# A transformer block on one core: powers of two moved to VectorE's PSUM bank, and the order of its start and end rebuilt

## What is computed

```
q, k, v = split(x @ Wqkv.T + bqkv)            # 16 heads of 16
q = elu(q * scale) + 1 ; k = elu(k * scale) + 1
y = q * cumsum(k * v) / max(sum_head(q * cumsum(k)), 1e-3)
x = layernorm(x + y @ Wproj.T + bproj)
h = gelu(bq(x) @ bq(w_fc).T + b_fc)           # 1024 wide
x = layernorm(x + bq(h) @ bq(w_proj).T + b_proj)
bq(v): blocks of 32; s = 2^(floor(log2(max|v|)) - 3); round(v / s) * s
```

## Time and profile before

| | us |
|---|---|
| median of 3 runs (lowest, highest) | 286.66 (284.94, 287.47) |
| the profiled execution, its own time | 287.42 |
| its span | 285.6 |
| VectorE busy | 242.0 (85%) |
| TensorE matmul busy | 245.0 (86%) |
| ScalarE, GpSimd busy | 146.4, 154.8 |
| TensorE's mean granted clock | 0.94 |
| chain that ended last | VectorE 52%, TensorE 24%, GpSimd 8%, DMA 8% |

### The profile page before, as it was taken

One profiled execution on the slowest core, in us unless ns is written; L12 is line 12 of the kernel. 1 busy time (PEld: TensorE's weight loads), 2 busy tenths in 40 slices (PEclk: granted clock), 3 DMA queues, 4 the chain that ended last, 5 costly groups with the idle time before them and its releaser, 6 DMA issues.

```text
span 285.6 us, 3556 instructions
## 1 busy us (share of the span) xinstructions
PE 245.0 (86%) x1156; PEld 143.7 (50%) x1156; DVE 242.0 (85%) x505; ACT 146.4 (51%) x238; POOL 154.8 (54%) x113
## 2 busy tenths in 40 slices
PE   6798897899999999999999999999999989276460
PEld 5544564564565546564656455645664456131230
DVE  1299699599999999999999999999999999848622
ACT  0662317465648564847484747475648554208002
POOL 1055154567628763876377647673676377627501
PEclk9999599999999999999999999999999999759666
DMA  6910020206320662066205720483055302530542
GB/s 165 364 60 3 0 55 21 39 0 147 73 39 0 157 138 40 0 147 147 39 0 117 161 56 1 72 187 73 0 54 134 72 1 40 146 73 0 110 110 73
DMA packets 55793, 22.26 MB, mean 78 GB/s; under 512 B 45280, under 2 KB 55520, under 8 KB 55776
## 3 DMA queue, kind: packets, MB, share of 16 engines
q1 hardware_dynamic: 54144, 21.77, 33.8%
q10 hardware_dynamic: 1632, 0.27, 0.6%
HBM read 7.35 MB, written 4.19 MB: 40 GB/s over the span
## 4 chain that ended last, share of the span: by engine, by line
DVE 52%; PE 24%; POOL 8%; DMA 8%; issue 4%; ACT 2%; SPq 1%; ACTq 0%; POOLq 0%; DVEq 0%
DVE vbank L788 10%; PE abank L1030 9%; DVE vbank L766 6%; PE dbank L1082 6%; DVE hq L703 6%; POOL num L352 4%; DMA h<-in_L_ffn_w_fc_dram 4%; DVE kvsum L744 3%; DMA xqT<-xq 3%; DVE r L760 3%; DVE vbank L778 3%; DVE r L800 3%; POOL rstd L357 2%; PE bbank L1041 2%; DVE y L756 2%
## 5 line engine op out<-in xcount | busy, mean ns | idle before, releaser
L1030 PE MATMUL abank<-xT,WqkvT 128*128 128x512 f32 x176 | 83.5, 610 | 5.7 <-DVE kf L727 4.0
L372 POOL TENSOR_TENSOR h_round<-h,h_inv 128x1024 f16<-128x1024 f32 x32 | 69.1, 2158 | 17.3 <-DVE h_inv L698 15.5
L504 ACT ACTIVATE h<-hbank 128x512 f32<-128x512 f32 x64 | 36.8, 600 | 65.2 <-PE hbank L1073 65.0
L1030 PEld LDWEIGHTS abank<-xT,WqkvT 128*128 128x128 f32 x176 | 31.6, 193 | 37.8 <-issue 23.8
L1082 PE MATMUL dbank<-w_prT,hT 128*128 128x256 bf16 x256 | 38.1, 299 | 7.9 <-DMA hT<-hq 7.8
L348 POOL TENSOR_TENSOR qk<-qf,ksum 128x512 f32<-128x512 f32 x16 | 22.6, 1413 | 31.0 <-DVE ksum L739 18.6
L788 DVE TENSOR_REDUCE vbank<-h 128x32 f32<-128x1024 f32 x32 | 38.9, 1214 | 0.5 <-ACT h L504 0.5
L1073 PE MATMUL hbank<-w_fcT,xqT 128*128 128x512 bf16 x128 | 38.3, 381 | 0.0
L498 ACT ACTIVATE expz<-abank,zbias_neg 128x512 f32<-128x512 f32 x30 | 20.6, 687 | 32.0 <-PE abank L1030 31.6
L357 POOL TENSOR_TENSOR rstd<-vareps,minus_half 128x4 f32<-128x4 f32 x16 | 16.1, 1008 | 36.2 <-DVE vareps L774 36.2
L1082 PEld LDWEIGHTS dbank<-w_prT,hT 128*128 128x128 bf16 x256 | 26.7, 106 | 17.4 <-DMA hT<-hq 9.5
(11 more groups left out here) (91 smaller groups left out, 347.9 us busy)
## 6 DMA issues: line engine op xcount, KB each, us to landing
x_sb<-in_L_attn_x_dram SPq DMA_DIRECT2D x8, 512.0 KB, 4.8
out_dram<-o_sb SPq DMA_DIRECT2D x7, 512.0 KB, 3.2
h<-in_L_ffn_w_fc_dram SPq DMA_DIRECT2D x1, 1024.0 KB, 10.3
h<-in_L_ffn_w_proj_dram SPq DMA_DIRECT2D x1, 1024.0 KB, 11.5
Wqkv_sb<-in_L_attn_Wqkv_dram SPq DMA_DIRECT2D x1, 512.0 KB, 6.6
hT<-hq SPq DMA_TRANSPOSE x32, 3.0
out_dram<-o_sb SPq DMA_DIRECT2D x4, 128.0 KB, 1.7
Wqkv_sb<-in_L_attn_Wqkv_dram SPq DMA_DIRECT2D x1, 256.0 KB, 7.0
```

Of the source, the lines that this page charges most:

```text
L372: nc.gpsimd.tensor_tensor(h_round[:, t % 2].rearrange("p (g j) -> p g j", j=BLOCK_K), h[:, t].rearrange("p (g j) -> p g j", j=BLOCK_K), h_ ...
L504: nc.scalar.activation(h[:, t, half * HALF:(half + 1) * HALF], hbank[half][:, :], ACT.Gelu).then_inc(s_h, 1)
L1030: last = nc.tensor.matmul(ps[:, :], WqkvT[:, k, e * P:(e + 1) * P], xT[:, k], start=(k == 0), stop=(k == CC - 1))
```

## The change

1. *Powers in PSUM.* `powers` gives way to `paired_powers` for x and h (the weights keep the old one): the exponent bits go once to SBUF (`x_exp`, `h_exp`), the inverse is made from them, and a third instruction multiplies them by 65537 into 32-bit words in `vbank`, each word two equal bf16. `times_power` reads these words as pairs of bf16. `quantise_x` and `quantise_h` wait for one more semaphore.
2. *Start.* q's and k's weights are loaded apart, k first; x is transposed first, then k's, q's; ScalarE runs one Exp on four elements before anything else; `split_biases` goes ahead of `w_exponents(0)`; `quantise_w(0)` and others change places; chunk 0's xq is turned by TensorE and copied by ScalarE.
3. *Order in the steady loop.* On VectorE, TensorE, ScalarE, GpSimd and SP's queue, as the diff shows.
4. *Last chunk.* LayerNorm 1, x's quantisation, LayerNorm 2 and the last stores go by halves of two tiles (new helpers `..._half`); xq and hq of chunk 7 are turned by TensorE and copied by ScalarE instead of by DMA; `residual_2(7, 1, 0)` waits for `norm_2(6)` explicitly.

The core of the diff (the written-out steps 5 and 6 follow the loop's pattern and are left out, the `_half` helpers are the old ones on two tiles):

```diff
-        x_pow = sb("x_pow", [P, TILES * XB, 2], BF16)
+        x_exp = sb("x_exp", [P, TILES * XB], BF16)
...
-        h_pow = sb("h_pow", [P, TILES, HB, 2], BF16)
+        h_exp = sb("h_exp", [P, TILES, HB], BF16)
...
+        x_pow, h_pow = vbank[:, 168:168 + TILES * XB], vbank[:, 360:360 + TILES * HB]
...
-            sp.dma_start(Wqkv_sb[:, 0:4], Wqkv_d[:, 0:4]).then_inc(s_wqk, 16)
+            sp.dma_start(Wqkv_sb[:, 2:4], Wqkv_d[:, 2:4]).then_inc(s_wk, 16)
+            sp.dma_start(Wqkv_sb[:, 0:2], Wqkv_d[:, 0:2]).then_inc(s_wq_in, 16)
             sp.dma_start(Wqkv_sb[:, 4:6], Wqkv_d[:, 4:6]).then_inc(s_wv, 16)
...
-            load(3)
             turn_hq(0, 2)
             turn_hq(0, 3)
-            turn_xq(1)
+            load(3)
 
             def step(s):
                 n = s + 1
+                turn_xq(n)
                 turn_hq(n, 0)
-                turn_hq(n, 1)
                 n = s
...
+                turn_hq(n, 1)
                 n = s + 4
                 load(n)
                 n = s + 1
                 turn_hq(n, 2)
...
-            turn_hq(7, 0)
-            turn_hq(7, 1)
-            turn_hq(7, 2)
-            turn_hq(7, 3)
             store(6)
...
                 n = s + 2
                 q_times_ksum(n, n % 2, 0)
                 n = s + 1
...
                 round_h(n, 2)
+                round_h(n, 3)
 
             for s in range(STEPS):
                 step(s)
...
             round_h(6, 2)
-            scale_shift_1(7)
             round_h(6, 3)
-            round_x(7, 1)
+            scale_shift_1_half(7, 0)
+            scale_shift_1_half(7, 1)
+            round_x_half(7, 1, 0)
+            round_x_half(7, 1, 1)
             scale_shift_2(6)
             round_h(7, 0)
             round_h(7, 1)
             round_h(7, 2)
             round_h(7, 3)
-            scale_shift_2(7)
+            scale_shift_2_half(7, 0)
+            scale_shift_2_half(7, 1)
...
+            def load_table():
+                act.wait_ge(s_half, 1)
+                nc.scalar.activation(table[:, :], minus_half[:, :], ACT.Exp).then_inc(s_table, 1)
...
+            def copy_xqT_first(n):
+                act.wait_ge(s_xqT_ps, 1)
+                nc.scalar.copy(xqT[:, :, :, :].rearrange("p t c n -> p (t c n)").bitcast(U32), hbank[0][:, :].bitcast(U32)).then_inc(s_xqT, 16)
+
+            def copy_xqT_half(n, g):
+                act.wait_ge(s_xqT_ps, g + 2)
+                nc.scalar.copy(xqT[:, 2 * g:2 * g + 2].rearrange("p t c n -> p (t c n)").bitcast(U32),
+                               abank[g][:, 0:C].bitcast(U32)).then_inc(s_xqT, 16)
+
+            def copy_hT(n, t):
+                slot = (4 * n + t) % HT
+                act.wait_ge(s_hT_ps, t + 1)
+                wait(act, s_down, 4 * n + t + 1 - HT)
+                nc.scalar.copy(hT[:, slot].rearrange("p c n -> p (c n)").bitcast(U32), abank[t % 2][:, :].bitcast(U32)).then_inc(s_hT[slot], 16)
...
+            load_table()
             copy_xT(0, 0, abank[0])
+            copy_wqkT(0, hbank[0])
+            copy_xT(0, 1, abank[1])
+            copy_wqkT(1, hbank[1])
+            activate(0, 1, 0, abank[0])
             copy_wvT()
-            copy_xT(0, 1, abank[1])
+            activate(0, 0, 0, hbank[0])
             copy_wprojT()
-            activate(0, 1, 0, abank[0])
-            activate(0, 0, 0, hbank[0])
             activate(0, 1, 1, abank[1])
             activate(0, 0, 1, hbank[1])
...
             def step(s):
                 n = s
+                gelu(n, 3, 0)
+                gelu(n, 3, 1)
+                n = s + 2
+                copy_xT(n, 0, abank[0])
+                copy_xT(n, 1, abank[1])
+                activate(n, 1, 0, abank[0])
+                activate(n, 0, 0, abank[1])
+                n = s + 1
+                norm_1(n, n % 2)
+                n = s + 2
+                activate(n, 1, 1, abank[1])
+                activate(n, 0, 1, abank[0])
+                n = s + 1
+                gelu(n, 0, 0)
+                gelu(n, 0, 1)
+                n = s + 2
+                widen_rec(n)
+                n = s + 1
+                gelu(n, 1, 0)
+                gelu(n, 1, 1)
                 gelu(n, 2, 0)
                 gelu(n, 2, 1)
-                gelu(n, 3, 0)
-                gelu(n, 3, 1)
-                n = s + 2
-                activate(n, 1, 0, abank[0])
-                activate(n, 0, 0, abank[1])
-                n = s + 1
-                norm_1(n, n % 2)
-                n = s + 2
-                activate(n, 1, 1, abank[1])
-                activate(n, 0, 1, abank[0])
-                n = s + 1
-                gelu(n, 0, 0)
-                n = s + 3
-                copy_xT(n, 0, abank[0])
-                n = s + 1
-                gelu(n, 0, 1)
-                n = s + 2
-                widen_rec(n)
-                n = s + 1
-                gelu(n, 1, 0)
-                gelu(n, 1, 1)
                 n = s
                 norm_2(n)
-                n = s + 3
-                copy_xT(n, 1, abank[1])
 
...
+            norm_1_half(7, 1, 0)
+            norm_1_half(7, 1, 1)
+            copy_xqT_half(7, 0)
             gelu(7, 0, 0)
             gelu(7, 0, 1)
             gelu(7, 1, 0)
+            copy_xqT_half(7, 1)
             gelu(7, 1, 1)
             gelu(7, 2, 0)
             gelu(7, 2, 1)
-            norm_2(6)
             gelu(7, 3, 0)
             gelu(7, 3, 1)
-            norm_2_last(7)
+            copy_hT(7, 0)
+            norm_2(6)
+            copy_hT(7, 1)
+            copy_hT(7, 2)
+            copy_hT(7, 3)
+            norm_2_half(7, 0)
+            norm_2_half(7, 1)
...
+            def paired_powers(amax, exp, inv, pow2, s_amax, s_exp, s_inv, s_pow, n):
+
+                top = amax.bitcast(U16).rearrange("p (g o) -> p g o", o=2)[:, :, 1]
+                wait(dve, s_amax, n)
+                nc.vector.tensor_scalar(exp.bitcast(U16), top, EXPONENT_BITS, None, ALU.bitwise_and).then_inc(s_exp, 1)
+                wait(dve, s_exp, n)
+                nc.vector.tensor_scalar(inv.bitcast(U16), exp.bitcast(U16), -1.0, float(TO_GRID), ALU.mult, ALU.add).then_inc(s_inv, 1)
+                nc.vector.tensor_scalar(pow2.bitcast(U32), exp.bitcast(U16), float((1 << 16) + 1), None, ALU.mult).then_inc(s_pow, 1)
...
                 nc.vector.tensor_reduce(h_amax[:, t], h[:, t].rearrange("p (g j) -> p g j", j=BLOCK_K), AX_X,
                                         ALU.max, apply_absolute_value=True).then_inc(s_hamax, 1)
-                powers(h_amax[:, t], h_pow[:, t], h_inv[:, t], HB, s_hamax, s_hexp, s_hinv, 4 * S + t + 1)
+                paired_powers(h_amax[:, t], h_exp[:, t], h_inv[:, t], h_pow[:, t * HB:(t + 1) * HB], s_hamax, s_hexp, s_hinv, s_hpow, 4 * S + t + 1)
 
             def quantise_h(S, t):
                 wait(dve, s_hround, 4 * S + t + 1)
-                times_power(hq[:, t], h_round[:, t % 2], h_pow[:, t], HB).then_inc(s_hq, 1)
+                wait(dve, s_hpow, 4 * S + t + 1)
+                times_power(hq[:, t], h_round[:, t % 2], h_pow[:, t * HB:(t + 1) * HB].bitcast(BF16).rearrange("p (g o) -> p g o", o=2), HB).then_inc(s_hq, 1)
...
+            split_biases()
             w_exponents(0)
-            split_biases()
...
 
             def step(s):
+                n = s + 1
+                mean_var_1(n)
                 n = s
-                h_exponents(n, 3)
-                quantise_h(n, 2)
                 residual_2(n, n % 2, 0)
+                quantise_h(n, 3)
                 n = s + 2
                 feature(n, 1, 0, abank[0])
                 sum_k(n, n % 2, 0)
                 feature(n, 0, 0, abank[1])
                 n = s
-                quantise_h(n, 3)
+                residual_2(n, n % 2, 1)
+                n = s + 1
+                x_exponents(n, n % 2)
                 n = s + 2
                 multiply_kv(n, 0, abank[0])
-                n = s + 1
-                x_exponents(n, n % 2)
-                n = s
-                residual_2(n, n % 2, 1)
-                n = s + 2
-                sum_kv(n, n % 2, 0)
-                feature(n, 1, 1, abank[1])
-                n = s + 1
-                quantise_x(n)
                 n = s
                 residual_2(n, n % 2, 2)
                 n = s + 2
+                feature(n, 1, 1, abank[1])
+                n = s + 1
+                quantise_x(n)
+                n = s + 2
+                sum_k(n, n % 2, 1)
+                n = s
+                residual_2(n, n % 2, 3)
+                n = s + 2
                 feature(n, 0, 1, abank[0])
-                sum_k(n, n % 2, 1)
+                sum_kv(n, n % 2, 0)
                 multiply_kv(n, 1, abank[1])
                 n = s
-                residual_2(n, n % 2, 3)
                 mean_var_2(n)
                 n = s + 2
...
             residual_1(7, 1, 0)
-            h_exponents(6, 2)
             quantise_h(6, 1)
+            h_exponents(6, 3)
             residual_1(7, 1, 1)
-            mean_var_1(7)
```

(102 more changed lines are left out.)

312 lines of the change are left out of this document (175 added, 137 removed).

## The result

The change is faster: a median of 272.6 us over four runs (271.57 to 275.36) against 287.07 over four runs of before (284.94 to 288.98), a ratio of 0.951, 95% interval 0.941 to 0.961. In a later series the same kernel gave 272.34 over six runs against 285.61 over ten, 0.953 (0.949 to 0.957). The forecast was 274. Ratios leave out the runs that are more than 1.5% above the fastest of their kernel, which matters in experiment 1 alone. The profiled execution took 271.57 us, the fastest of its four; its span is 269.8: 15.8 us less than the 285.6 of before, where the medians differ by 14.5.

A forecast was written before the change was run, and what follows sets the result against it. VectorE and TensorE were taken to fill the middle steps, with idle time only at both ends. Gains of 6 (start), 0 (middle) and 7 (end) make 13 us off 287.42; with the median 0.76 lower, forecast 274, range 269 to 278.

The forecast's parts named there:

- the second y: Start, projection behind the denominators: done 4.4 us earlier than 35.3 if TensorE's clock falls again, 6.5 if not.
- w_fc's landing and 3.1 us of VectorE work set the start, not PE: Start: k is projected in time, so the first `feature` can start at 15.8, 4.1 us earlier.
- The tight place at the inverse of the next chunk's first tile: Middle step: VectorE's inverse would come while GpSimd still multiplies by kvsum, losing 0.4 us.
- claim (d): Theory stated before the experiments: the middle's 0.25 us loss a step is the third instruction and the blocked inverse.
- The other place, `x_exponents`: Middle step: comes 3.8 us after LayerNorm 1's statistics, now 6.3, leaving a margin of 0.2 us.
- the rival at 292.6 us: Multiply with a PSUM operand falls to one element per cycle, +0.53 us each, 18.6 us in all; chance 0.13.
- GpSimd's 0.38 us: Each of some 27 GpSimd roundings gets 0.38 us shorter with powers in PSUM; priced at nothing in the middle.
- To the end of down(7,0): End, from first product to first down: 5.0 us now, 3.7 to 4.6 new, about 0.8 gained.
- The 1.7 us that the forecast took off for the clock: End: terms summed to 8.7 us gained, taken as 7 because TensorE's clock might be at its lower level.
- The middle gives back: Rival: waits at `x_exponents` and the inverse, or an unoverlapped third instruction, cost 1.1 us a step, 280.6 us; chance 0.17.
- The ends gain little: Rival: lower TensorE clock through both ends, start 4 and end 4 us gained, 278.7 us; chance 0.13.
- It doesn't do what it says: Rival: `h_round` stays at 2.28 us, colliding with the exponents' SBUF instructions, not the multiply; 275.5 us; chance 0.05.

The follow-up runs named there:

- experiment 1: Kernel before with only the bias split moved ahead of `w_exponents(0)` on VectorE: 286.17 us against 286.50, ratio 0.994.
- experiment 5: Kernel before with only the powers of x and h moved to PSUM as 32-bit words, every order kept: 286.85 us, ratio 1.002.
- experiment 2: Kernel after with the bias split put back behind `w_exponents(0)`: 279.51 us.
- experiment 4: Kernel after with chunk 0's xq turned by DMA instead of by TensorE transposes and a ScalarE copy: 279.06 us.
- experiment 7: Kernel after with the exponents too as 32-bit words in PSUM: 270.32 us; repeated in one series, 270.30 against 272.34 us of after.
- experiment 6: Kernel after with the powers of x and h back in SBUF, every order as after: 303.92 us, ratio to before 1.063.

## Why the prediction was right, point by point

**The bound.** Three stretches, a middle at capacity and two ends: right. All of the gain is in the ends. That the total came so close owes something to luck: by the profiles the gain of the two ends was forecast 4.6 us too small (2.5 and 2.1), the middle 1.8 us too good, and the start's 8.5 lies outside its own range of 4 to 8.

**Start (-6 forecast, -8.5 measured).** The places were right within 0.4 us: `feature` at 15.8 (15.45), k projected from 9.5 (9.29), denominators at 22.4 (22.28). What was too low was the sum behind them. I had priced the second y at 4.4 us if the clock falls and 6.5 if not, and took a value between; it didn't fall, and the y came 6.8 us earlier. Where the clock doesn't fall in before either (experiment 5), the gain is 6.3. For xqT I gave 1.5 us, "part of it hidden": `xq` to `up` went from 3.3 us to 1.6, nothing of it hidden, and 6.8 + 1.7 is the 8.5. Experiments 2 and 4 show what each is worth inside the new order: 6.7 and 3.5 us, more than their durations: the idle stretches of TensorE that they bring back, 2.74 and 2.14 us, are followed by matmuls at the lower level. And experiment 1 shows what the forecast left unsaid: moved alone, the split gives 0.3 to 1.8 us. The step "so w_fc's landing and 3.1 us of VectorE work set the start, not PE" holds only with TensorE's new order beside it.

**Middle (0 forecast, +1.8 measured).** The third instruction is +0.05 a block, +0.18 to 0.25 a step, as worked out (experiment 5). The tight place at the inverse of the next chunk's first tile was named, with its 0.4 us: it took 0.49 in chunks 1 and 3 to 6, and experiment 7 takes it away. So the two causes of claim (d) are there, but they are more than the 0.25: 0.18 for the third instruction and 0.35 by experiment 7 make 0.53 a step. The 0.28 between is what the new order gives back by the difference; no run shows it alone. The other place, `x_exponents`, never waited. The one step of 30.44 us in the profiled run isn't there in the second profile of the same kernel, whose middle is 176.8: +1.3. Both lie inside the bounds of -2 and +3; 29.2 as the likeliest step was 0.3 low, since the inverse's 0.4 was put into the range and not into the sum.

**The product.** `hq` stays at 0.68 us with the power in PSUM, so the rival at 292.6 us is out. Here two places of the Trainium skill, named in the prediction, stand against each other, and the measurement decides. That 1024 elements take 0.676 us, where a reduction of 1024 takes 1.22, speaks for the Trainium skill's "Vector Engine (DVE) Microarchitecture Reference", section 5.1, and against the entry for a PSUM operand in the `tensor_tensor` row of the perf-mode tier table of its "VectorE: DVE Perf Modes", for 16-bit pairs of this form.

**What the powers are for.** The forecast priced GpSimd's 0.38 us at nothing in the middle; experiment 5 agrees. It didn't see the larger thing: a product that starts behind a rounding waits for its end (experiment 6). The rows that showed it were in the prediction, the bias subtraction of 3.47 us and the inverse of 0.59, and they were used for the start and for the inverse, not for the product. Had the powers stayed in SBUF, the result would have been 303.9 us, and the forecast had no rival for that.

**End (-7 forecast, -9.1 measured).** From chunk 6's mark to 7's: 21.3 forecast, 22.6 measured, and 21.5 to 24.7 over the other profiles with this order and the powers in PSUM. The rows of after show one cause: downs of 1.91 us at 239.95, at the lower level of the clock, which the 21.3 had not counted, and 1.7 us in which VectorE waits for them. No experiment takes back the halves of this stretch, so what they bring is argued, not shown. To the end of the first product 4.1 us (4.36 measured). To the end of down(7,0): 0.8 gained by the forecast, 2.5 measured; this is the mis-sized term. I had the transposes and the copy behind the last `up`, at 3.7 to 4.6 us; TensorE was free in time and all of it took 2.45. The four downs, 8.3 us before, took 7.9 (6.4 to 9 forecast); down(7,1) stood behind `norm_2(6)` as worked out (the 2.07 us at 255.01). Statistics and normalisation gave 2.1 (1.8). The 1.7 us that the forecast took off for the clock were not needed behind chunk 7's mark, where it is 0.91.

**The rivals.** "The middle gives back" has its mechanism in part, at under a quarter of its price: 0.25 us a step and not 1.1. "The ends gain little" fell: TensorE stays at the upper level through the whole start, and behind chunk 6's mark the granted clock is 0.85 and 0.91. "It doesn't do what it says" fell with experiment 5: the roundings take 1.90 us as soon as the products read their powers from PSUM, with the exponents' other operands still in SBUF.

## What to carry to other kernels

When several limits of about the same height meet at one point, price a change with both taken away and also with each alone: here the bias split is worth 1.8 us at most in one order and 6.7 in the other, and the powers in PSUM 0 and 31. In these runs VectorE's 16-bit product, its small inverse and the 12-element subtraction, all operands in SBUF, were cheap unless they started behind GpSimd's rounding or one of its products by the sums, for whose end they then waited; so look at which of the two starts first at each place before an order is changed. And the idle stretches of TensorE that experiments 2 and 4 brought back cost more than their length, since the matmuls on the chain came behind them at the lower level; whoever closes such a stretch gains both.

## What the runs showed of the hardware that I had not expected

- Who starts first decides. `hq` at 121.64, GpSimd's rounding 0.17 us behind it: 0.68 us, and the rounding takes 2.3 to 2.4 instead of 1.90. `hq` 0.44 us behind a rounding: 2.01 us, and the rounding keeps its 1.90 (experiment 6). With one operand in PSUM neither loses anything (experiment 5). VectorE's reciprocal doesn't wait either: 0.55 us with its operands in SBUF, started at 30.59 inside GpSimd's product of 30.52 to 31.79 (experiment 1).
- A 12-element subtraction and a 32-element inverse wait for GpSimd in the same way as a product of 1024 elements: 3.47 instead of 0.17 us, 0.66 instead of 0.17. With its input in PSUM the inverse took 0.190 to 0.192 in all 32 cases (experiment 7).
- After 1.02 us of idle at the same place of the start, TensorE's clock fell in the profile of before and not in that of experiment 5; after the 0.18 of the new order it fell in none of eight. That is 2.2 us of difference between two executions with the same order.
- The lower level of TensorE's clock made a start of the denominators that was 1.8 us late into 3.5 us of delay (experiment 4), and one that was 4.3 us late into 6.7 (experiment 2).
